# Image tower, one core: query and key columns loaded once, features as 32-row products in four row tiles

## The reference

```python
h = conv2d(x, stem_w, stem_b, 4)                      # 96 channels, 24 x 24
h = leaky_relu(batchnorm(h, ...))
offset = conv2d(h, off_w, off_b, 4)                   # 32 channels, 6 x 6
h = deform_conv(h, offset, dcn_w, dcn_b)              # 16 taps, 4 corners each, 192 channels
h = leaky_relu(batchnorm(h, ...))                     # 36 tokens an image

def _phi(t, random_features):
    norm_sq = 0.5 * jnp.sum(t * t, axis=-1, keepdims=True)
    proj = jnp.einsum('bhnd,md->bhnm', t, random_features)
    return jnp.exp(proj - norm_sq) * (1.0 / math.sqrt(M))   # M = 64, 12 heads of 16

q_p = _phi(q, random_features)
k_p = _phi(k, random_features)
kv = jnp.einsum('bhnm,bhnd->bhmd', k_p, v)
out = jnp.einsum('bhnm,bhmd->bhnd', q_p, kv)
out = out / (normalizer + 1e-06)
h = h + _layernorm(h + out @ W_proj + b_proj)         # x is the layernormed h inside
h = h + experts(_layernorm(h))                        # 3 experts, the chosen one times its score
```

## Time and profile before

| | before |
|---|---|
| median of 3 runs | 481.15 us (479.4 to 483.73) |
| profiled execution, its own time | 481.56 us |
| profiled execution, span | 479.7 us |
| PE / DVE / ACT / POOL busy | 85% / 62% / 47% / 33% |

### The profile page before, as it was taken

How to read it: one execution, slowest core, us unless ns; L and a number is a source line. 1 busy time by engine, 2 the same in 40 slices (tenths; PEclk the granted TensorE clock), 3 DMA queues, 4 the chain that set the end, 5 groups by cost and what they waited for, 6 DMA issues and landing times.

```text
span 479.7 us, 7764 instructions
## 1 busy us (share of the span) xinstructions
PE 408.9 (85%) x2630; PEld 288.5 (60%) x2630; DVE 295.5 (62%) x1128; ACT 227.1 (47%) x548; POOL 158.4 (33%) x168
## 2 busy tenths in 40 slices
PE   3894377699987899899897997899897979989997
PEld 2473244555763587658575873557575845857575
DVE  2562457745359679763698858463699876367213
ACT  2473256333567764427438435327447532742520
POOL 3114677301756550026466410035466300000000
PEclk9995578759996699999999996699999999999999
DMA  5549955589745231395345300295344300000000
GB/s 129 155 112 250 222 177 153 166 271 242 223 118 152 77 101 33 74 223 170 99 135 161 107 17 2 58 245 159 99 133 118 100 1 1 1 0 10 11 1 18
DMA packets 60022, 54.27 MB, mean 113 GB/s; under 512 B 44242, under 2 KB 52335, under 8 KB 59983
## 3 DMA queue, kind: packets, MB, share of 16 engines
q1 hardware_dynamic: 50336, 25.42, 20.8%
q0 software_dynamic: 9216, 28.32, 20.7%
q10 hardware_dynamic: 431, 0.03, 0.1%
HBM read 38.70 MB, written 15.06 MB: 112 GB/s over the span
## 4 chain that ended last, share of the span: by engine, by line
PE 65%; ACT 10%; DVE 10%; POOL 6%; issue 6%; DMA 2%; ACTq 1%; DVEq 0%; POOLq 0%
PE bank L925 10%; PE bank L897 7%; POOL ring L531 6%; PE bank L613 5%; PE bank L904 5%; PE bank L594 4%; PE bank L688 4%; PE bank L624 4%; PE bank L812 3%; PE bank L831 3%; PE bank L816 2%; PE bank L772 2%; PE bank L566 2%; DMA ring<-cells,cell 2%; PE bank L929 2%
## 5 line engine op out<-in xcount | busy, mean ns | idle before, releaser
L531 POOL DMA_INDIRECT ring<-cells,cell x144 | 146.1, 1014 | 192.9 <-DVE cell L1369 67.6
L1391 DVE SCALAR_TENSOR_TENSOR bank<-ring,corner,bank 128x96 f32<-128x96 f32 x224 | 52.9, 311 | 17.7 <-ACT bank L1102 17.6
L1228 ACT ACTIVATE hid<-bank,b_up 128x288 f32<-128x288 f32 x72 | 32.0, 498 | 61.3 <-PE bank L904 61.2
L688 PE MATMUL bank<-w_dcn,shared 128*128 128x192 f32 x192 | 43.8, 370 | 13.8 <-ACT shared L1111 13.8
L925 PE MATMUL bank<-w_down,hid 128*128 128x192 f32 x288 | 52.1, 332 | 0.0
L897 PE MATMUL bank<-xfT,w_up 128*128 128x288 f32 x144 | 45.2, 438 | 5.5 <-ACT hid L1228 5.2
L925 PEld LDWEIGHTS bank<-w_down,hid 128*128 128x128 f32 x288 | 46.2, 190 | 4.6 <-issue 4.4
L688 PEld LDWEIGHTS bank<-w_dcn,shared 128*128 128x128 f32 x192 | 34.2, 207 | 22.4 <-ACT shared L1111 18.5
L1102 ACT ACTIVATE bank<-ring,corner 128x96 f32<-128x96 f32 x112 | 31.4, 334 | 15.0 <-DMA ring<-cells,cell 15.0
L897 PEld LDWEIGHTS bank<-xfT,w_up 128*128 128x128 f32 x144 | 25.6, 197 | 14.1 <-ACT hid L1228 7.6
L594 PE MATMUL bank<-xt,w_stem 48*96 48x384 f32 x96 | 31.6, 762 | 1.2 <-DVE h L1408 1.2
(11 more groups left out here) (186 smaller groups left out, 672.5 us busy)
## 6 DMA issues: line engine op xcount, KB each, us to landing
cells<-ring SPq DMA_DIRECT2D x16, 864.0 KB, 9.6
xs<-in_x_dram SPq DMA_DIRECT2D x28, 108.0 KB
ring<-cells,cell POOLq DMA_INDIRECT x144, 3.2
w_down<-in_L_ffn_W_dram SPq DMA_DIRECT2D x3, 576.0 KB, 6.9
hid<-in_L_tok_dcn_w_dram SPq DMA_DIRECT2D x1, 1152.0 KB, 7.9
w_up<-in_L_ffn_W_dram SPq DMA_DIRECT2D x3, 384.0 KB, 3.6
out_dram<-y SPq DMA_DIRECT2D x8, 96.0 KB, 2.1
w_up_rest<-in_L_ffn_W_dram SPq DMA_DIRECT2D x6, 96.0 KB, 3.9
```

What stands on the lines that cost most here:

```text
L531: pool.indirect_dma_start(ring[:, ring_slot(k), j, :], None, table[0:HALF_CELLS, :] if k < EARLY else table, bass.IndirectOffsetOnAxis(ap= ...
L688: mm = pe.matmul(tokens_out(t), samp[:, n % 2, i, :], w_dcn[:, CHUNKS * (k % QUADS) + i, :], start=(k % QUADS == 0 and i == 0), stop=(k % ...
L1228: act.activation(hid[:, e % 2, f, :], up_bank(g, n)[:, 0:TOK], ACT.Gelu, bias=b_up[:, n:n + 1]).then_inc(gelu_done, 1)
L1391: ins = dve.scalar_tensor_tensor(acc[:, k % 3, :, j, :] if c == 3 else part_sum, ring[:, ring_slot(k), j, C1 * c:C1 * (c + 1)].rearrange(" ...
```

## The change

- Query and key columns stand once: three 128-column blocks n = 0, 1, 2 (n = 0 and half of 1 are queries, the rest keys) in banks 4 to 6 instead of six double blocks of 64. The weights are loaded by three DMAs of whole rows.
- All 128-row products of queries, keys and values come first, then all 64-row parts, alternately in the two halves of the array; values get banks 0 to 2. Waits for the banks stand ahead of the first product.
- DVE copies whole blocks, keys first; ACT squares the copy, no longer the bank. A small exponential at the start of `squares` brings in the table early.
- Features are products over 32 rows, in four row tiles (`quad(r)`), each pair of heads with its own tile and bank: part 0 with the channels, part 1 adds the squares. Keys come first (pairs 2 to 5 in banks 4 to 7, then 0 and 1 in banks 2 and 3), then the queries.
- The exponentials read several banks in one instruction: four for keys, three for queries.
- `sample_points` ends with the cell indices; the corner weights stand in `sample_corners`, behind `values`.
- `kv_sums` waits for the values instead of the tenth exponential; POOL's pause at batch 2 waits for the fourth of seven exponentials.
- The random features are loaded eight times instead of four; head masks have another shape.

```diff
@@ -135,15 +137,15 @@
-        headmask = sb("headmask", [64, 4 * M])
+        headmask = sb("headmask", [128, 2 * M])
...
-        w_qk = sb("w_qk", [128, 6, 2, 64])
-        w_qk_rest = sb("w_qk_rest", [128, 3, 2, 64])
+        w_qk = sb("w_qk", [128, QK, 128])
+        w_qk_rest = sb("w_qk_rest", [128, QK, 128])
...
-        w_feat = sb("w_feat", [128, 4 * M])
+        w_feat = sb("w_feat", [128, 2, 2 * M])
...
-            for d in range(2):
-                sp.dma_start(w_qk[:, :, d, :], w["W_qkv"][0:WIDE, 0:2 * C2].rearrange("p (n c) -> p n c", c=64)).then_inc(ld_attn, 16)
+            sp.dma_start(w_qk[:, :, :], w["W_qkv"][0:WIDE, 0:2 * C2].rearrange("p (n c) -> p n c", c=128)).then_inc(ld_attn, 16)
             for i in range(2):
-                for d in range(2):
-                    sp.dma_start(w_qk_rest[lower(i), :, d, :],
-                                 w["W_qkv"][WIDE:C2, 0:2 * C2].rearrange("p (q i c) -> i p q c", i=2, c=64)[i]).then_inc(ld_attn, 16)
+                sp.dma_start(w_qk_rest[lower(i), :, :],
+                             w["W_qkv"][WIDE:C2, 0:2 * C2].rearrange("p (n c) -> p n c", c=128)).then_inc(ld_attn, 16)
...
                 elif k == 2:
-                    pool.wait_ge(exp_done, 12 * (g - 1) + 10)
+                    pool.wait_ge(exp_done, EXPS * (g - 1) + 4)
...
-            def qkv(g, has_next):
+            def qk_wide(g, n):
+
+                pe.matmul(qk_bank(n)[:, 0:TOK], w_qk[:, n, :], lnT[:, 0, :], start=True, stop=False)
+
+            def qk_rest(n, i):
+
+                pe.matmul(qk_bank(n)[:, 0:TOK], w_qk_rest[lower(i), n, :], lnT[lower(i), 1, :],
+                          start=False, stop=True).then_inc(qk_mm, 1)
+
+            def value_wide(t):
+                t0, n = TILES[t]
+                pe.matmul(ps[t][0:n, 0:C2], lnT[:, 0, t0:t0 + n], w_v[:, 0, :], start=True, stop=False)
+
+            def value_rest(t, i):
+                t0, n = TILES[t]
+                pe.matmul(ps[t][0:n, 0:C2], lnT[lower(i), 1, t0:t0 + n], w_v[lower(i), 1, :],
+                          start=False, stop=True).then_inc(v_mm, 1)
+
+            def qkv(g, has_last, has_next):
+
+                if has_last:
+                    pe.wait_ge(gelu_done, 18 * (g - 1) + 12)
+                    pe.wait_ge(y_added, 9 * (g - 1) + 1)
+                if has_next:
+                    pe.wait_ge(bn_evac, bn_done(g + 1, 12))
+                    pe.wait_ge(xt_evac, 6 * (g + 2))
                 pe.wait_ge(t2_evac, 3 * g + 1)
-                query_key(g, 0, has_next)
-                value(g, 0, 2)
-                query_key(g, 1, has_next)
-                value(g, 2, 3)
-                query_key(g, 2, has_next)
+                qk_wide(g, 2)
+                qk_wide(g, 1)
+                if has_next:
+                    pe.wait_ge(idx_chain, 11 * (g + 1) + 1)
+                else:
+                    pe.wait_ge(y_added, 9 * (g - 1) + 5)
+                qk_wide(g, 0)
+                pe.wait_ge(t2_evac, 3 * (g + 1))
+                for t in (2, 0, 1):
+                    value_wide(t)
+                qk_rest(2, 0)
+                qk_rest(1, 1)
+                qk_rest(0, 0)
+                value_rest(2, 1)
+                value_rest(0, 0)
+                value_rest(1, 1)
...
+            def k_features(t, pairs, first):
+
+                t0, n = TILES[t]
+                for part in range(2):
+                    for i, p in enumerate(pairs):
+                        r, c = (6 + p) % 4, (6 + p) // 4
+                        mm = pe.matmul(ps[first + i][0:n, 128 * t:128 * t + 128], qk[quad(r), QK * part + c, t0:t0 + n],
+                                       w_feat[quad(r), part, :], start=(part == 0), stop=(part == 1), skip_group_check=True)
+                return mm
+
+            def q_features(pairs, first):
+
+                for part in range(2):
+                    for i, p in enumerate(pairs):
+                        r = p % 4
+                        mm = pe.matmul(ps[first + i][:, 0:TOK], w_feat[quad(r), part, :], qk[quad(r), QK * part + p // 4, :],
+                                       start=(part == 0), stop=(part == 1))
+                        if part == 1 and i % 2 == 1:
+                            mm.then_inc(feat_mm, 1)
 
             def features(g):
 
+                pe.wait_ge(q_copied, QK * (g + 1))
+                pe.wait_ge(q_squared, QK * g + 1)
+                for t in range(3):
+                    mm = k_features(t, (2, 3, 4, 5), 4)
+                mm.then_inc(feat_mm, 1)
+                pe.wait_ge(q_squared, QK * g + 2)
+                pe.wait_ge(v_evac, 3 * g + 1)
+                for t in range(3):
+                    mm = k_features(t, (0, 1), 2)
+                mm.then_inc(feat_mm, 1)
+                pe.wait_ge(q_squared, QK * g + 3)
+                pe.wait_ge(exp_done, EXPS * g + 2)
+                q_features((0, 1, 2, 3), 4)
+                pe.wait_ge(exp_done, EXPS * g + 4)
+                q_features((4, 5), 2)
+
...
+            def kv_sums(g):
...
+                    if u == 2:
+                        pe.wait_ge(exp_done, EXPS * g + 5)
...
             def squares(g):
-                for n in range(6):
-                    act.wait_ge(qk_mm, 6 * g + n + 1)
-                    act.activation(qk[64:128, n, :], ps[2 + n % 3][64:128, 0:TOK], ACT.Square).then_inc(q_squared, 1)
+                act.activation(prob[:, 0:1], ident[0:GROUP, 0:1], ACT.Exp)
+                for i, n in enumerate((2, 1, 0)):
+                    act.wait_ge(q_copied, QK * g + i + 1)
+                    act.activation(qk[:, QK + n, :], qk[:, n, :], ACT.Square).then_inc(q_squared, 1)
+
+            def q_exps(g, n, first, p):
+
+                act.wait_ge(feat_mm, FEATS * g + n)
+                act.activation(qp[:, p:p + 2, :], banks[:, first:first + 2, 0:TOK], ACT.Exp).then_inc(exp_done, 1)
+
+            def k_exps(g, n, tiles, first, p, count):
+
+                act.wait_ge(feat_mm, FEATS * g + n)
+                a, rows = tiles[0], TILES[tiles[0]][1]
+                b = a + len(tiles)
+                act.activation(kp[0:rows, a:b, 128 * p:128 * (p + count)].rearrange("t a (p f) -> t p a f", p=count),
+                               banks[0:rows, first:first + count, 128 * a:128 * b].rearrange("t p (a f) -> t p a f", f=128),
+                               ACT.Exp).then_inc(exp_done, 1)
 
             def exps(g):
-                for u in range(12):
-                    act.wait_ge(feat_mm, 12 * g + u + 1)
-                    bank = ps[u % 4]
-                    if u < 6:
-                        n = TILES[u // 2][1]
-                        w0, w1 = (0, 512) if u % 2 == 0 else (512, 768)
-                        act.activation(kp[0:n, u // 2, w0:w1], bank[0:n, 0:w1 - w0], ACT.Exp).then_inc(exp_done, 1)
-                    else:
-                        act.activation(qp[:, u - 6, :], bank[:, 0:TOK], ACT.Exp).then_inc(exp_done, 1)
+                for n, first, p, count in ((1, 4, 2, 4), (2, 2, 0, 2)):
+                    k_exps(g, n, (0, 1), first, p, count)
+                    k_exps(g, n, (2,), first, p, count)
+                q_exps(g, 3, 4, 0)
+                q_exps(g, 4, 6, 2)
+                q_exps(g, 5, 2, 4)
 
...
-            for i in range(4):
+            for i in range(8):
                 act.dma_start(feat_nat[:, i, :], w["random_features"]).then_inc(ld_nat, 16)
...
                 dve.tensor_tensor(cell[:, :], cell_f[:, :], rowbase[:, :], ALU.add).then_inc(idx_ready, 1)
+
+            def sample_corners(g):
+
+                chain = Chain(dve, idx_chain, g, 11, 8)
                 chain.link(dve.tensor_scalar(hat[:, :, 1], hat[:, :, 0], -1.0, None, ALU.add))
...
-            def q_copies(g, first, last):
-                for n in range(first, last):
-                    dve.wait_ge(qk_mm, 6 * g + n + 1)
-                    dve.tensor_copy(qk[0:64, n, :], ps[2 + n % 3][0:64, 0:TOK]).then_inc(q_copied, 1)
-
-            def values(g, first, last):
-
-                for t in range(first, last):
+            def q_copies(g):
+                for i, n in enumerate((2, 1, 0)):
+                    dve.wait_ge(qk_mm, QK * g + i + 1)
+                    dve.tensor_copy(qk[:, n, :], qk_bank(n)[:, 0:TOK]).then_inc(q_copied, 1)
+
+            def values(g):
+
+                for i, t in enumerate((2, 0, 1)):
                     n = TILES[t][1]
-                    dve.wait_ge(v_mm, 3 * g + t + 1)
+                    dve.wait_ge(v_mm, 3 * g + i + 1)
                     for i in range(n // TOK_IMG):
                         dst = mv[0:n, t, i, :].rearrange("t (h c) -> t h c", c=VW)[:, :, 0:DH]
-                        ins = dve.tensor_scalar(dst, ps[t % 2][0:n, 0:C2].rearrange("t (h c) -> t h c", c=DH),
+                        ins = dve.tensor_scalar(dst, ps[t][0:n, 0:C2].rearrange("t (h c) -> t h c", c=DH),
                                                 own[0:n, i:i + 1], None, ALU.mult)
```

(22 more changed lines are left out.)

85 lines of the change are left out of this document (28 added, 57 removed).

## The result

| | before | after |
|---|---|---|
| median | 482.44 us (4 runs, 479.4 to 484.16) | 462.69 us (4 runs, 459.83 to 465.01) |
| profiled execution, its own time | 481.56 us | 459.83 us |
| span | 479.7 us | 458.0 us |
| mean granted clock of TensorE | 0.915 | 0.929 |

The changed kernel is faster: ratio 0.9594, 95% interval 0.9518 to 0.9671. The forecast was 461.0 us, in a range of 455 to 471.

A forecast was written before the change was run, and what follows sets the result against it. TensorE was taken to bound each group's attention from query/key products to key-value sums. Terms -22.4 + 0.9 + 2.3 - 1.3 = -20.5 took the profiled 481.56 us to 461.1, given as 461, range 455 to 471.

The forecast's parts named there:

- K-T: Per image group, first wide query/key product (T) to first key-value sum (K): from 15.50 to 9.85 us.
- The row-tile rate: Feature products on TensorE: four 32-row tiles run side by side at full rate, 0.108 us a part-round; called the weakest term.
- The rival of two tiles at a time: Features: only two of four row tiles run together; 3.45 us gained a group, 470 us; chance 0.11.
- One after the other: Features: 32-row products run serially, attention 2.9 us later than before a group, 495 us; chance 0.03.
- The gathers: Rival: POOL's gathers become the bound, groups 0 to 2 gain nothing, 477 us; chance 0.05.
- DVE, ACT and the table: Work beside TensorE's attention path: corner weights, copies, exponentials and the moved 1.28 us table load cost nothing.
- Start-up, +2.3: Four more feature-matrix loads in ACT's queue ahead of its first copy delay the stem by 2.3 us.
- Weight loads, -1.3: 256 query/key weight pieces instead of 2,304 shorten POOL's 2.07 us wait for corners by two thirds, 1.3 us.
- POOL's copy in group 0, +0.9: POOL's input rows for group 2, wanted at T+15.0, come at T+15.9, so TensorE's transposes wait 0.9 us.
- the main term: Attention start of every group, first wide product to key-value sums: 5.6 us less a group, 22.4 in all.
- The clock: Rival: half-clock stretches behind attention cost 6.8 us each, 27 in all four groups, 488 us; chance 0.05.

The follow-up runs named there:

- e8: Changed kernel with each four-pair feature set issued as two sets of two pairs; 466.19 us median, ratio 0.971.
- e2: Changed kernel with DVE's corner weights put back ahead of the query/key copies and the values; 461.47 us.
- e3: Changed kernel without the small early exponential, so the table is loaded ahead of the first key exponential; 463.94 us.
- e11: e9 with fewer throwaway products per pause and 5 more ahead of L634; 514.55 us in a disturbed session (kernel before: 504.86), not used.
- e6: Changed kernel with the loops over part and pairs exchanged in both feature functions; K-T 10.30 us, no total time given.
- e7: Changed kernel with wide products and 64-row parts alternating again; 465.4 us.
- e10: The changed kernel, unaltered, profiled a second time; 461.28 us median.
- e1: Changed kernel with its eight loads of the random features made one broadcasting load; 458.32 us median, ratio 0.957.
- e5: Changed kernel with query/key weights loaded twice again, in 64-column pieces; 460.51 us.
- e9: e1 plus throwaway products in TensorE's pauses during the stem of groups 2 and 3; 460.13 us median.
- e12: The kernel of e11 run once more, on another chip; 456.89 us median, ratio 0.9538.

## Why the prediction was right

**K-T: 5.65 us less foreseen (15.50 to 9.85; 5.6 in the sum), 5.41 measured.** The 64-row parts begin at T+2.63, as worked out, and TensorE is through with them at T+4.19, the tail of the last record included (foreseen 4.12). The first copy begins at T+3.41: I had the first two blocks complete at T+3.1 and forgot the time from a last record's start to its result, so the copies end at T+4.60 in place of 4.3, features start at T+4.66 in place of 4.4, and the wait ahead is 0.47 in place of 0.3. ACT starts at T+6.30 (5.95), is through after 1.51 (1.55), and TensorE waits 0.40 for it (0.4). Key features and that wait take 3.29 (3.1), query features and the last switch 2.14 (2.35); these two errors cancel, so the 0.24 missing are the late copies.

**The row-tile rate.** All four row tiles run at full rate: in the first key set four records start 0.007 us apart, and the rounds follow every 0.109 us, as do the rounds of two tiles in the second set. 72 key records take 2.89 us; 24 rounds of 0.108 are 2.6, and the rest is the time to the second round and the tail of the last.

The trace disagrees with the Trainium skill ("TensorE: Matmul & The Clock Gate", Part 3), whose 3.07x for four row tiles would by an estimate have made the rounds of the first key set last 1.3 times as long.

The rival of two tiles at a time is out by the rounds of four, and e8 is 0.94 us a group slower in spite of its overlap. One after the other is out too. The gathers did not become the bound: the groups with gathers behind them kept their 5.4 us, and no stretch behind attention grew by more than 0.5.

**DVE, ACT and the table.** Costed at nothing, and e2 confirms it for the corner weights. The place of the table load is worth 0.09 us a group by e3, which I had at 0.

**Start-up, +2.3.** Right: 2.19 at the first copy, 2.1 at T0 on average, with a scatter of T0 that is larger.

**Weight loads, -1.3.** Wrong. I took two thirds of one wait of 2.07 us for the price of the pieces; in two profiles of the kernel before that wait is 2.07 and 1.14, and in two of the changed one 1.77 and 3.40. The packets did get fewer (queue 1 took 10,784 in 33 us, has 12,880), the wait didn't get shorter.

**POOL's copy in group 0, +0.9.** Mechanism right, size off, and not one that one execution can give. It starts at 131.04, T+14.5, and TensorE waits for it:

```profile
132.37 0.54 PE L580 MATMUL bank<-ident_sb,xr 96*112 96x96 f32 x4 [0.34 <-POOL xr L500]
```

0.34 us, since TensorE came there at T+15.5, 0.5 later than foreseen. In the other profiles of changed kernels but e11's this wait is nothing (e2, e6, e7, e10), 0.58 (e1), 0.99 (e8) and 2.0 to 2.4 us (e3, e5, e9, e12); the four longest all have T0 below 115 us. What an early start gains can so be lost again here, and this wait, with the length of the half-clock stretch, is most of the scatter of K0 to T1.

**What no term had.** K1 to T2 is 2.4 us shorter, by the shorter half-clock stretch. K2 to T3 is 0.48 us longer in both profiles of the changed kernel (68.89, 68.84 against 68.41, 68.49). Laid side by side, 0.10 of it stand right behind K, in every group: the second key-value record starts 0.19 us after the first in place of 0.09, now that products in another tiling stand ahead of it. Another 0.13 are a longer wait for DVE ahead of the transposes (L771, 0.53 in place of 0.39), and 0.09 one for ACT ahead of T3 (0.59 in place of 0.50); for the last 0.16 no wait is named.

**Luck in the number.** The sum is -21.7 against -20.5 foreseen. Term by term it is further off: the start came out 1.6 worse (+2.63 in place of +1.0: the 1.3 of the weight loads, and scatter), the attention starts 0.9 worse and the last two stretches 0.6 worse; K1 to T2 came out 2.4 better, and K0 to T1 1.8 better (0.9 shorter where 0.9 longer was foreseen). That these nearly cancel, and that the forecast of 461.0 stands 1.2 above the profiled execution and 1.7 below the median, is luck. Not luck is the main term, 21.5 of 22.4, with the path that was given for it. The clock was a rival on the side of slower; between T and K no profile but e11's shows half clock. It changed the time all the same, elsewhere and in the other direction.

## What to carry to other kernels

Products of few rows are worth spreading over all four row tiles: here, with each tile writing its own bank, a round of four cost what one costs, and four records of one tile in a row cost only 0.21 us a group more. Price an edit at the issue queue (0.6 us for each small DMA ahead of the first compute) as carefully as one in the main loop, and don't price a wait that you have seen once: profile the kernel before twice, and compare the two profiles stretch by stretch. Where TensorE runs at half clock, look at its short pauses ahead of that stretch before looking at the products in it.

## What was not expected of the hardware

- Records of other row tiles start behind a busy one: four records of one tile in a row instead of alternating tiles cost 0.21 us a group (e6).
- A record of 64 columns with 128 rows and 128 weight columns held TensorE 0.116 us (e9), no less than one of 128 columns on 32 rows (0.109).
- Pauses of 1.24 and 1.78 us, with TensorE busy 14.3 (e10: 14.5) of the 17.6 us ahead, were followed by 10.2 us at the 1.2 GHz level in both profiles of the changed kernel; with the pauses filled (15.7 of 16.0 us busy, e12) it didn't come.
